# An audio tower with a product-key lookup: the dot products of a unit as 16 fused multiply-and-sum instructions

## The reference, cut to what matters

```python
s, idx = jax.lax.top_k(sub_scores, K)                  # K = 8, 8 heads
best_s, best_pos = jax.lax.top_k(all_scores, K)
indices = jnp.take_along_axis(all_idx, best_pos, axis=-1)
w_down = w_down_embed[indices]
w_up = w_up_embed[indices]
x = jnp.einsum('nd,nhkd->nhk', q_tok, w_down)          # the dots
x = jax.nn.gelu(x)
vals = x * jax.nn.softmax(best_s, axis=-1)
out = jnp.einsum('nhk,nhkd->nd', vals, w_up)
```

## Time and profile before

| | us |
|---|---|
| median of 3 runs | 5308.14 |
| lowest and highest run | 5295.98 and 5309.39 |
| span of the profiled execution, first to last instruction | 3653.6 |
| median of the runs less that span | 1654.5 |
| POOL busy, first gather to last | 2630.0 |
| DVE busy | 2446.6 |
| PE busy | 2636.7 |

### The profile page before, as it was taken

One profiled execution on the slowest core, in us unless ns is written; L12 is line 12 of the kernel. 1 busy time (PEld: TensorE's weight loads), 2 busy tenths in 40 slices (PEclk: granted clock), 3 DMA queues, 4 the chain that ended last, 5 costly groups with the idle time before them and its releaser, 6 DMA issues.

```text
span 3653.6 us, 46237 instructions
## 1 busy us (share of the span) xinstructions
PE 2636.7 (72%) x10589; PEld 1663.4 (46%) x10631; DVE 2446.6 (67%) x9145; ACT 1736.6 (48%) x4864; POOL 2630.0 (72%) x2772
## 2 busy tenths in 40 slices
PE   4455768777776878777686767778676777868588
PEld 2132435444454545445453544445454444535366
DVE  4456676676777766677767667676766777776653
ACT  1323454444545544454554545455544555455454
POOL 3777777777777777777777777777777777777740
PEclk7567788777887877788888878888887788888788
DMA  2234333343434344343434434333443333343320
GB/s 98 81 107 109 107 109 107 110 111 106 110 106 110 106 110 110 107 110 107 109 106 110 111 107 109 107 109 106 110 106 111 110 107 109 106 110 107 106 66 4
DMA packets 155365, 378.88 MB, mean 104 GB/s; under 512 B 50602, under 2 KB 66860, under 8 KB 154924
## 3 DMA queue, kind: packets, MB, share of 16 engines
q0 software_dynamic: 135168, 358.12, 35.7%
q1 hardware_dynamic: 20012, 19.10, 1.7%
HBM read 368.62 MB, written 2.79 MB: 102 GB/s over the span
## 4 chain that ended last, share of the span: by engine, by line
POOL 69%; issue 23%; PE 5%; DVE 1%; ACT 1%; DMA 0%; POOLq 0%; SPq 0%; DVEq 0%; ACTq 0%
POOL ring L457 69%; PE bank_x L680 1%; PE bank_x L676 1%; PE bank_s L525 1%; PE bank_l L610 0%; PE bank_u L534 0%; PE bank_l L618 0%; PE bank_l L606 0%; DMA ring<-in_table_dram,idx 0%; ACT ht L922 0%; PE bank_l L572 0%; DVE xu L1219 0%; POOLq L453 0%; PE bank_l L585 0%; ACT vx L810 0%
## 5 line engine op out<-in xcount | busy, mean ns | idle before, releaser
L457 POOL DMA_INDIRECT ring<-in_table_dram,idx x2752 | 2627.6, 955 | 892.3 <-issue 891.4
L861 ACT ACTIVATE ring<-ring,vu 128x128 f32<-128x128 f32 (+1 forms) x2752 | 820.8, 388 | 95.0 <-DVE vu L1235 94.8
L534 PE MATMUL bank_u<-ring,ident 128*128 128x512 f32 (+1 forms) x1376 | 743.0, 690 | 113.7 <-ACT ring L861 113.7
L1216 DVE TENSOR_TENSOR ring<-ring,bank_q 128x1024 f32<-128x1024 f32 (+1 forms) x344 | 403.9, 1215 | 583.3 <-DMA ring<-in_table_dram,idx 565.0
L676 PE MATMUL bank_x<-z3t,w_s 128*128 128x255 f32 (+1 forms) x1408 | 425.6, 436 | 216.0 <-ACT ht L922 216.0
L534 PEld LDWEIGHTS bank_u<-ring,ident 128*128 128x128 f32 (+1 forms) x1376 | 301.5, 225 | 453.9 <-issue 320.1
L922 ACT ACTIVATE ht<-bank_x,b_s 128x255 f32<-128x255 f32 (+1 forms) x704 | 288.5, 462 | 401.9 <-PE bank_x L676 400.7
L676 PEld LDWEIGHTS bank_x<-z3t,w_s 128*128 128x128 f32 x1408 | 291.2, 218 | 314.2 <-ACT ht L922 231.8
L1219 DVE TENSOR_REDUCE xu<-ring 128x8 f32<-128x1024 f32 (+1 forms) x344 | 402.0, 1209 | 0.0
L680 PE MATMUL bank_x<-ht,w_s 128*128 128x255 f32 (+1 forms) x1408 | 332.2, 378 | 21.9 <-ACT ht L922 21.9
L855 ACT ACTIVATE th<-xu 128x16 f32<-128x16 f32 (+1 forms) x172 | 37.2, 216 | 580.6 <-DVE xu L1227 579.8
(11 more groups left out here) (200 smaller groups left out, 3473.7 us busy)
## 6 DMA issues: line engine op xcount, KB each, us to landing
ring<-in_table_dram,idx POOLq DMA_INDIRECT x2752
w_s<-in_w_dram SPq DMA_DIRECT2D x2, 2048.0 KB
x_s<-in_xg_dram SPq DMA_DIRECT2D x21, 191.2 KB, 4.1
out_dram<-acc SPq DMA_DIRECT2D x21, 127.5 KB
h1p<-h SPq DMA_DIRECT2D x43, 42.5 KB
h<-h2p SPq DMA_DIRECT2D x43, 42.5 KB
ring<-in_pq_w_dram SPq DMA_DIRECT2D x1, 512.0 KB, 3.3
ring<-in_pkeys_dram SPq DMA_DIRECT2D x1, 512.0 KB, 4.2
```

The source lines that it names most:

```text
L457: pool.indirect_dma_start(ring[0:rows, u, k, :], None, table, bass.IndirectOffsetOnAxis(ap=idx[0:rows, j, c:c + 1], axis=0)).then_inc(gath ...
L534: ins = mm(U[0:rows, :], ident[0:rows, 0:rows], ring[0:rows, u, 4 * c:4 * c + 4, D:ROW], start=(u == 0 and c == 0), stop=(u == UNITS - 1 a ...
L861: ins = act.activation(up, up, ACT.Copy, scale=vu[0:rows, u, k:k + 1])
L1216: ch.did(tt(w, w, qrep[r, j, :].unsqueeze(1).to_broadcast([rows, half, D]), ALU.mult))
```

## The change

The two multiplies and the two row sums of a unit are replaced by 16 instructions of one slot each. Each multiplies the 128 `w_down` values of a slot by `qrep`, writes the product back in place, and sums it into one element of `xu`. Nothing waits between the 16, and one wait stands behind the last. `U_STEPS` grows from 7 to 19 accordingly, and a `sem_inc` on `carried`, a semaphore that nobody waits for, stands ahead of the first.

```diff
-        A_STEPS, T_STEPS, U_STEPS, L_STEPS, R_STEPS = 18, 76, 7, 55, 13
+        A_STEPS, T_STEPS, U_STEPS, L_STEPS, R_STEPS = 18, 76, 19, 55, 13
...
-                half = UR // 2
-                for i in range(2):
-                    w = ring[r, u, i * half:i * half + half, 0:D]
-                    ch.did(tt(w, w, qrep[r, j, :].unsqueeze(1).to_broadcast([rows, half, D]), ALU.mult))
-                for i in range(2):
-                    ch.wait(1)
-                    ch.did(dve.tensor_reduce(xu[r, 0, i * half:i * half + half], ring[r, u, i * half:i * half + half, 0:D],
-                                             AX.X, ALU.add))
+                dve.sem_inc(carried)
+                for k in range(UR):
+                    w = ring[r, u, k, 0:D]
+                    ch.did(dve.tensor_tensor_reduce(w, w, qrep[r, j, :], 1.0, 0.0, ALU.mult, ALU.add, xu[r, 0, k:k + 1]))
                 ch.wait()
```

## The result

| | kernel before | changed kernel | ratio (95% interval) |
|---|---|---|---|
| runs of the result, median | 5308.8 us | 5446.4 us | 1.0253 (1.0231 to 1.0276) |
| span of the profiled execution | 3653.6 us | 5447.3 us | |

The change made the kernel 2.5% slower; the forecast was no measurable change.

The account below looks back on a forecast made before the run. POOL's gather stream, one per 1.25 us, was taken to bound the kernel and hide the dots; 5308.1 us less 0.4 behind the last gather gave 5307.7 us, no measurable change (0.82), range about 5290 to 5335.

Parts of the forecast that it names:

- The base of the sum: Whole run: the 1654.5 us by which the runs' median exceeds the 3653.6 us span was assumed to stay unchanged.
- The path: 172 units: 69 us less DVE work, nearly all hidden by POOL's gathers; only the last unit's 0.4 us shows.
- gained or lost 0: POOL's stream of gathers: its 3465 us stay the same, since POOL does not wait for DVE.
- The room of 8.0 and 9.8 us: Before POOL's gathers: slots free 8.0 us early and indices ready 9.8 us early in the tightest tiles.
- Rival 1: DVE's dots become late, POOL waits for slots or indices: +38 us, 5346, at 0.65 us per pair; chance 0.04.
- Rival 3: Time outside the span paced by DVE at every unit: 69 us faster, 5239, up to 241 us; chance 0.06.
- Rival 2: Fused instructions or sum write-outs block gathers beside the dots: +58 us (5366) up to +199 us; chance 0.08.
- The price of a pair: Unit's dots on DVE: each fused instruction with its write-out 0.26 us, 16 pairs 4.2 us, 0.4 us shorter per unit.
- my low end: Unit's dots: write-out costs nothing, 16 x 0.195 + 0.1 = 3.2 us, a unit 1.4 us shorter.
- the MAX8 row: Profile row of eight MAX8 of 128 elements in 1.64 us, giving 0.195 us between multiplying parts.
- the load-and-find row: Profile row alternating short and 128-element instructions: load to find 0.06 us, load to next load 0.26, taken as pair price.
- The estimate from the page "VectorE: DVE Perf Modes": Unit's dots: 0.26 us per main part, 0.06 per write-out, 5.1 us a unit, half a microsecond slower than now.

Follow-up runs that it names:

- e7: Changed kernel with the dots left out, one write of a constant in place of the 16 fused instructions: 3659.9 us, 1.0010 to the kernel before, fast pace.
- The padding: Kernel before with 28 one-element writes added to each unit on VectorE, nothing else changed; at the slow pace 5563.7 us against 5298.6, ratio 1.0504.
- e5_changed: The changed kernel, unchanged, run again at the fast pace: 3659.0 us against 3654.5 for the kernel before, ratio 1.0009.
- e2_pad: Kernel before with 28 one-element writes added to each unit on VectorE, run at the fast pace: 3660.2 us, ratio 1.0012.

## Why the prediction was wrong

**The base of the sum.** The step that failed is "I carry it unchanged": 1654.5 us between the profile and the runs were taken for time without instructions, and called an assumption. All executions for which both are on record have 1.7 to 1.8 us there. The right reading of a span 31% below the time was that the profile does not show the execution that was timed. The forecast then held for the pace of the profile (1.0009) and not for that of the runs, where the change cost 138 us (1.0253).

**The path.** At the profile's pace POOL's stream was the bound, and that part was right point by point: gathers 1.25 us apart, DVE's wait for them grown by 183 us where 172 x 1.19 = 205 us were saved, dots that are worth nothing even when they vanish (e7). At the slow pace the statement "gained or lost 0" fails: POOL waits 1778 us, for the slots and the indices as far as the waits are named. The room of 8.0 and 9.8 us that I had counted is gone there. The prediction put no cost on the number of instructions itself, beyond their time on DVE; there, 4816 more of them without any use cost 265 us.

**Rival 1** had the right waits, `bank_u` and the index, and the wrong cause: the median unit is 3.46 us, so the pair itself is as cheap as at the fast pace. The units that take 9.5 us and more, up to 35, are those in a slow stretch, in which other instructions are as late. **Rival 3** had a part of the truth, that the timed runs are paced by something DVE takes part in, but looked for it outside the span and had the wrong sign. It priced what DVE's work lasts; at the slow pace the number of its instructions costs too. 172 x 1.19 = 205 us less work came with 4816 more instructions, and the sum was +138 us in one set and +171 in the other. The padding had the same number with 52 us more work: +265. If both terms were simply proportional, 257 us of work would be worth 94 to 127 us and the instructions alone about 240 to 246 us, 0.05 us each. That is an estimate from three measurements in two sets. It leaves out that the change adds increments and the padding none, and the uneven units above say that the place may count as well.

**Rival 2** did not happen: gathers beside the fused instructions take 0.946 us on average, as beside the wide ones. It happens once the row lies in SBUF.

**The price of a pair** was mis-sized: 4.2 us a unit forecast, 3.46 measured. The end of the last unit's dots in e5_changed:

```profile
3533.76 0.28 DVE L1216 CUSTOM_DVE_ANT_0 ring<-ring,bank_q 128x128 f32<-128x128 f32 x1
3533.97 0.08 DVE L1216 DVE_READ_ACCUMULATOR2_ANT xu<- 128x1 f32 x1
3534.08 0.17 DVE L1219 TENSOR_TENSOR xu<-xu 128x16 f32<-128x16 f32 x1
```

The first fused instruction starts at 3530.63, so the unit is 3.45 us, against 4.64. The multiplying parts follow 0.208 us apart, and each write-out starts together with the next one. It is almost hidden, as in my low end, and adds 0.013 us to the 0.195 of the MAX8 row, not the 0.06 of the load-and-find row. The estimate from the page "VectorE: DVE Perf Modes" of the Trainium skill, 0.26 us from one multiplying part with a PSUM source to the next, is too high here (one lasts 0.28 us by itself, but the next starts after 0.208); the measurement decides.

**What stays open.** What makes a set of runs go at 5300 us, and what DVE and SyncE wait for in the stretches of 0.7 and 1.4 us, is not shown. Two rivals are left. One is how instructions are supplied: SyncE's register instructions are slowed as well, and the queue that carries instructions moves more for a longer VectorE list: of the kernel before and of e5_changed,

```profile
q14 instruction: 167, 1.37, 0.1%
```
```profile
q14 instruction: 192, 1.57, 0.1%
```

(packets, MB), with 192 in the slow traces too. The counts are no proof, and one thing speaks against it: a packet of this queue takes 0.44 us on average in the slow trace of the result and 0.45 in e5_changed. The other rival is the recording. Every execution on record, timed or profiled, has a recorded span, and at the slow pace two thirds of the records of semaphore increments are missing (17881 to 18676 in the three slow traces, 58338 to 60626 in those of before, e2_pad and e5_changed). If the recording held the engines up, its cost would grow with the number of instructions, as it does here; whether the missing records are the cause or another effect, and whether the program takes 5300 us unrecorded, no run tells. The slow pace came unforeseen and in two sets only, so the variants with fewer instructions or fewer increments were never measured in it.

## What to carry to other kernels

Compare the profile's span with the time of the runs before anything else (here 1.7 to 1.8 us apart when they belong together); if they differ by more than a few us, the profile is of another execution than the one to be forecast, and no slack read from it can be counted on. An engine with room at one pace may set the end at another, so cutting its work into many instructions is a risk even where each piece is cheap: here 32 took 3.46 us instead of 4.64 for four, and the kernel lost 2.5% at one pace and nothing that could be measured at the other. Where GpSimd issues gathers all the time and sets the end, keep one input of the long two-input VectorE instructions in PSUM: for the wide multiplies that alone was worth 2.1%.

## What had not been expected of the hardware

- The same program takes 3655 or 5300 us, for a whole set of runs, with VectorE's and GpSimd's instructions as long as ever; on one chip (3) both were met.
- At the slow pace VectorE and SyncE start instructions 0.7 or 1.4 us apart, register instructions among them, in stretches (1033 and 202 such starts, against 131 and 42 at the fast pace); TensorE and ScalarE do not (76 and 107, against 48 and 145).
- At the slow pace VectorE's semaphore increments come late: it is idle for 1237 us before instructions that wait only for its own earlier ones, against 119 us.
- A fused multiply-and-sum of 128 elements, with its write-out, follows the last after 0.208 us.
- Leaving out 798 us of VectorE's work made the program no faster at the fast pace (1.0010 and 1.0003), since the stream of gathers sets its time.
